# A signal of its own for the gate half of every up step in a macaron block on one core

## The chip, the cores and the metric

The kernel runs on one core of a Trainium2 chip. Time is device time of one execution, in microseconds (us). The engines of the core run side by side and meet only through semaphores: TensorE (PE) multiplies, ScalarE (ACT) and VectorE (DVE) work on what it leaves in PSUM, GpSimd (POOL) does small things here, SyncE (SP) issues most transfers.

## What is computed

The block is a feed-forward, an attention and the same feed-forward again, each behind a layer norm and with a residual, on 4096 tokens of 512 features in fp32. Cut to what matters (einsums written short):

```python
def _L0_ffn_ref(x, W1, W2, W3):            # hidden width 2048
    up_gate = x @ W1.T
    up_lin = x @ W3.T
    hidden = silu(up_gate) * up_lin
    hidden = fwht(hidden)                  # Walsh-Hadamard over 2048
    return hidden @ W2.T

x = x + 0.5 * _L0_ffn_ref(_layernorm(x), W1, W2, W3)
x = x + _L0_attn_ref(_layernorm(x), wq, wk, wv, wo, inv_freq)
x = x + 0.5 * _L0_ffn_ref(_layernorm(x), W1, W2, W3)
```

The attention mixes the 16 heads of one token with each other (16 x 16 scores for a token), so no token looks at another one.

## The kernel before

**Tiles and passes.** A tile is 512 tokens, so there are 8 tiles, and each goes twice through the feed-forward. These are the 16 passes of `PASSES`, p = 0 to 15. Pass 0 (`first_pass`) also builds the weights, with the Hadamard transform folded into W2. Passes 1 to 15 are `feed_forward(p)` on every engine, and between two of them lies a gap (`first_gap`, `early_gap`, `late_gap`, and for the last pass `last_gap` on DVE), in which PE makes queries, keys, values and attention outputs for one to three blocks of 128 tokens.

**A step.** A pass has 16 steps of 128 hidden features, n = 0 to 15, with two buffers each, u = n % 2. In an *up step* PE makes both halves of a step in PSUM: `w = 0` is the gate, in bank `gu[:, 2u]`, and `w = 1` is the linear half, in bank `gu[:, 2u+1]`. Every product is three matmuls (`products`, lines 583 to 585: high by high, high by low, low by high, to get fp32 out of the fast format), so with 4 blocks of the contraction a half is 12 matmuls and a step 24. Then ACT computes silu of the gate into `gated` (L1031; L976 in pass 0), DVE multiplies `gated` by the linear half in place (L1525; L1407), ACT copies the product as the high part into `hid` (L1039), and DVE takes the low part as the difference (L1532). In a *down step* PE multiplies high and low by W2 into the four banks of `acc` (L614, L615 and L618; in the last down step of a pass by `products`).

**Order.** The order on each engine is written out by hand. On PE it is up(n), down(n-1), up(n+1), down(n), so that a down step lies between the end of an up step and the next. On DVE the two feed-forward instructions of a step stand in a row with everything else that it does: units of attention (a product over 1024 elements, L1258 or L1263, and a sum, L1270 or L1272), norms, and the shift and the sums of the softmax (L1278, L1279, L1286, L1287). On ACT the exponential of the softmax (L955) stands between the silu and the copy of some steps; silu and exponential each need their table loaded (ACT_TABLE_LOAD).

**Semaphores around the change.** `s_up_done` counts up steps: the last matmul of a step, of the half w = 1, raises it. ACT's silu waits for it and for the buffer `gated` to be free; SP's loads of the next up weights wait for it; in pass 0, so does the split of the next raw weights on ACT. DVE's product waits for `s_silu` alone. `s_h` counts the products, `s_hid_hi` and `s_hid_lo` the two parts. PE waits for `s_h` of two steps before it writes over a pair of banks in `gu`.

**The end of a pass.** Step 15 has no attention unit. Where the next pass's new tile is prepared beside this one, DVE does behind L1532: the low part of new blocks (L1138), two subtractions on the new tile's input (L1510), and then in the gap `add_sum` (L1202: residual plus `acc`) for s = 0, the statistics of one new block, `add_sum` for s = 1 to 3 and the block's norm (L1174). In the gaps of passes 2, 9 and 11 the second new block isn't ready earlier, and PE transposes it (L664) between the query and the key product of the first, as soon as that norm is there. In the other gaps both blocks were normed in the pass before.

Of the kernel before, what the change touches and what calls it, by code (L numbers as in the profile page):

```python
# [246 lines left out]
def build(nc, x, up_raw, w2t, attn_raw, inv_freq, hadamard, identity, out):  # L247
    ctx = ExitStack()
    with ctx:
# [3 lines left out]
        def sem(name):  # L253
            return ctx.enter_context(nc.semaphore(name))
# [65 lines left out]
        s_w_hi = sem("s_w_hi")  # L320
        s_wattn = sem("s_wattn")

        s_up_done = sem("s_up_done")
        s_silu = sem("s_silu")
        s_h = sem("s_h")
# [39 lines left out]
        def raw_hidden(n):  # L365

            at = RAW.index(n)
            if at < 2 * SUBS:
                return xs[2 + at // SUBS][:, at % SUBS, :]
            return prod[:, 2, (at - 2 * SUBS) * TOK:(at - 2 * SUBS + 1) * TOK]  # L370
# [21 lines left out]
        def residual(t):  # L392

            return xs[t % 4]
# [24 lines left out]
        def by_token(ap):  # L419
            return ap.rearrange("p (s q j) -> p s q j", s=SUBS, q=QUADS)  # L420

        def from_bank(ap, p):

            if p in MOVED:
                return ap.rearrange("p (q s j) -> p s q j", q=QUADS, s=SUBS)
            return by_token(ap)
# [153 lines left out]
        def _(pe):  # L580
            def products(o, w_hi, w_lo, m_hi, m_lo, first, last):

                nc.tensor.matmul(o, w_hi, m_hi, start=first, stop=False)  # L583
                nc.tensor.matmul(o, w_hi, m_lo, start=False, stop=False)  # L584
                return nc.tensor.matmul(o, w_lo, m_hi, start=False, stop=last)  # L585

            def split_ready(*key):

                pe.wait_ge(s_tp_lo, TP[key] + 1)

            def up(u, X, key=None):
                for w in range(2):
                    for k in range(KT):
                        if key == NP - 1:
                            if (w, k) == (0, 0):
                                for s in range(SUBS):
                                    split_ready("z", s, 0)
                        elif key in MOVED:
                            if w == 0 and k % 2 == 0:
                                pe.wait_ge(s_moved_lo, 2 * MOVED[key] + k // 2 + 1)  # L600
                        elif key is not None and w == 0:
                            split_ready("x", key, k)
                        ins = products(gu[:, 2 * u + w, :], w_up[:, u, 0, w, k, :], w_up[:, u, 1, w, k, :],
                                       X[:, 0, k, :], X[:, 1, k, :], k == 0, k == KT - 1)
                ins.then_inc(s_up_done, 1)

            def down(n, u, first, last, slab=None, split=None):
                hi, lo = (w_down[:, u, 0, :], w_down[:, u, 1, :]) if slab is None else slab
# [284 lines left out]
            for s in range(SUBS):  # L893
                pe.wait_ge(s_ln, s + 1)
                for k in range(KT):
                    ins = nc.tensor.transpose(gu[:, k, s * P:(s + 1) * P], xs[2][:, s, k * P:(k + 1) * P], ident[:])
# [15 lines left out]
        def _(act):  # L912
# [54 lines left out]
            up_high(1, 0, 1, False)  # L967
            for n in range(HT):
                u = n % 2
                act.wait_ge(s_up_done, n + 1)  # L970
                if n >= 2:
                    if n - 2 < SPLIT_FIRST:
                        act.wait_ge(s_hid_lo, n - 1)
                    else:
                        act.wait_ge(s_h, n - 1)
                nc.scalar.activation(gated[:, u, :], gu[:, 2 * u, :], ACT.Silu).then_inc(s_silu, 1)  # L976
                if n + 2 < HT:
                    up_high(n + 2, n // 2 + 1, u, True)
                for part, a in hadamard_batch(n):
                    act.wait_ge(s_had_ps, HT * part + a + 1)  # L980
                    nc.scalar.activation(down_stage[:, a, PARTS[part]], acc[:, a % BATCH, PARTS[part]], ACT.Copy, scale=DOWN_SCALE)\
                        .then_inc(s_down_hi, 1)
                if n < SPLIT_FIRST:
                    act.wait_ge(s_h, n + 1)
                    nc.scalar.activation(hidden_0(n)[0], gated[:, u, :], ACT.Copy).then_inc(s_hid_hi, 1)
                if n == 2:
                    act.dma_start(tok[:, :, W2_CUTS[2]], w2t[:, :, W2_CUTS[2]].rearrange("a p n -> p a n")).then_inc(s_w2[2], 16)
# [36 lines left out]
            def feed_forward(p):  # L1024

                n0, after = HT * p, p + 1
                for n in range(HT):
                    u = n % 2
                    act.wait_ge(s_up_done, n0 + n + 1)
                    act.wait_ge(s_hid_lo, n0 + n - 1)  # L1030
                    nc.scalar.activation(by_token(gated[:, u, :]), from_bank(gu[:, 2 * u, :], p), ACT.Silu).then_inc(s_silu, 1)  # L1031
                    for g in EXP_AHEAD.get((p, n), ()):
                        exp(g)
                    if n == HT - 1 and after == NP - 1:
                        for s in range(2):
                            block_high("o", s, (after + 1) % 2)
                    act.wait_ge(s_h, n0 + n + 1)
                    act.wait_ge(s_down_done, n0 + n - 1)
                    nc.scalar.activation(hidden(u)[0], gated[:, u, :], ACT.Copy).then_inc(s_hid_hi, 1)  # L1039
                    if n == HT - 1 and after < NP and after not in LATE:  # L1040
                        for g in early_subs(after):
                            sub_high(g)
                    for g in EXP_BEHIND.get((p, n), ()):
                        exp(g)
                    if after in MOVED and X_MOVE <= n < X_MOVE + QUADS:
                        move(after, n - X_MOVE)
                    if after in MOVED and n == X_SPLIT:
                        moved_high(after)
                    f, t = PASSES[p - 1]
                    if f == 2 and n == 1:  # L1050
                        act.wait_ge(s_added, SUBS * p)
                        act.dma_start(out_v[t], residual(t)[:]).then_inc(s_out, 16)
                    if f == 2 and n == 4 and t + 4 < TILES:
                        act.wait_ge(s_out, 16 * (t + 1))
                        act.dma_start(residual(t + 4)[:], x_v[t + 4]).then_inc(s_x[t % 2], 16)
# [67 lines left out]
        def _(dve):  # L1123
# [280 lines left out]
            for n in range(HT):  # L1404
                u = n % 2
                dve.wait_ge(s_silu, n + 1)
                nc.vector.tensor_tensor(raw_hidden(n) if n in RAW else gated[:, u, :], gated[:, u, :], gu[:, 2 * u + 1, :], ALU.mult)\  # L1407
                    .then_inc(s_h, 1)
                turn(1)
                if n + 2 < HT:  # L1410
                    up_low(n + 2, u)
                for part, a in hadamard_batch(n):
                    at = HT * part + a
                    dve.wait_ge(s_down_hi, at + 1)
                    cols = PARTS[part]
                    nc.vector.scalar_tensor_tensor(down_stage[:, a, D + cols.start:D + cols.stop], acc[:, a % BATCH, cols], DOWN_SCALE,
                                                   down_stage[:, a, cols].bitcast(FP32), ALU.mult, ALU.subtract).then_inc(s_down_lo, 1)
                if n < SPLIT_FIRST:
                    dve.wait_ge(s_hid_hi, n + 1)
                    high, low = hidden_0(n)  # L1420
                    nc.vector.tensor_tensor(low, gated[:, u, :], high.bitcast(FP32), ALU.subtract).then_inc(s_hid_lo, 1)
                turn(1)
# [41 lines left out]
            def feed_forward(p):  # L1464

                n0, after = HT * p, p + 1
# [55 lines left out]
                for n in range(HT):  # L1522
                    u, count = n % 2, len(STEP_UNITS[p][n])
                    dve.wait_ge(s_silu, n0 + n + 1)
                    nc.vector.tensor_tensor(by_token(gated[:, u, :]), by_token(gated[:, u, :]), from_bank(gu[:, 2 * u + 1, :], p), ALU.mult).then_inc(s_h, 1)  # L1525
                    unit(min(count, 1))
                    if n == HT - 1 and after == NP - 1:
                        for s in range(2):
                            block_low("o", s, (after + 1) % 2)
                    dve.wait_ge(s_hid_hi, n0 + n + 1)  # L1530
                    high, low = hidden(u)
                    nc.vector.tensor_tensor(low, gated[:, u, :], high.bitcast(FP32), ALU.subtract).then_inc(s_hid_lo, 1)  # L1532
                    unit(count - min(count, 1))
                    if n == HT - 1 and next_x:
                        for g in early:
                            sub_low(g)
                    beside(n)
# [144 lines left out]
```

## Time and profile before

| | us |
|---|---|
| runs before | 2517.53, 2519.74, 2520.30 |
| median | 2519.74 |
| the profiled execution | 2519.57 |
| its span | 2517.8 |
| outside the span | 1.8 |
| PE busy | 2504.8 |
| DVE busy | 2027.5 |
| ACT busy | 528.8 |

The mean granted clock of TensorE over the span is 0.999 of full speed. A row of matmuls shows each of them as about 0.39 us long while the next one begins 0.227 us after it, since they overlap; what counts is the distance from one start to the next. The idle time that the profile gives for PE begins only at the modelled end of the matmul before.

### The profile page before, as it was taken

To read this page: it belongs to the slowest core of one execution; us is meant where nothing else is said; L and a number is where in the kernel's file an instruction comes from. 1 tells how busy PE (TensorE), PEld (TensorE's weight loads), DVE (VectorE), ACT (ScalarE), POOL (GpSimd) and SP (SyncE) were. 2 spreads that over 40 slices of the span, in tenths; PEclk is the share of its full clock that TensorE was granted. 3 is DMA by queue.
4 is the path that set the end of the run, shared out by engine and by line. 5 is a ranking of instruction groups with operands and counts; after the bars stand their busy time and mean duration, and the time that the engine had idled before them with its cause. 6 is when DMAs were issued, how large, how long until landed. Compare 5 with 4: busy or idle time off the path is not lost.

```text
span 2517.8 us, 30105 instructions
## 1 busy us (share of the span) xinstructions
PE 2504.8 (99%) x11223; PEld 2074.0 (82%) x11223; DVE 2027.5 (81%) x2588; ACT 528.8 (21%) x810; POOL 63.6 (3%) x111
## 2 busy tenths in 40 slices
PE   9999999999999999999999999999999999999999
PEld 7878888888888888888888888888888888888887
DVE  9558978799786997979969889697886988978711
ACT  3322221222121221122212222122221212211211
POOL 0030000000000000000000000000000000000000
PEclk9999999999999999999999999999999999999999
DMA  9644635256452454525625546354562545535364
GB/s 340 251 188 177 213 138 190 101 199 202 169 207 76 176 210 162 203 100 200 203 89 208 167 180 211 118 213 146 200 208 76 186 165 210 185 115 200 134 219 165
DMA packets 112404, 446.89 MB, mean 177 GB/s; under 512 B 11201, under 2 KB 36033, under 8 KB 79041
## 3 DMA queue, kind: packets, MB, share of 16 engines
q1 hardware_dynamic: 82080, 420.26, 45.8%
q10 hardware_dynamic: 30240, 25.57, 3.4%
q8 instruction: 47, 0.77, 0.1%
q14 instruction: 37, 0.29, 0.0%
HBM read 402.79 MB, written 33.55 MB: 173 GB/s over the span
## 4 chain that ended last, share of the span: by engine, by line
PE 95%; DVE 4%; DMA 1%; ACT 0%; issue 0%; SPq 0%; DVEq 0%; ACTq 0%
PE gu L583 21%; PE gu L584 21%; PE gu L585 21%; PE acc L615 8%; PE acc L614 8%; PE acc L618 8%; PE acc L583 2%; PE acc L585 2%; PE acc L584 2%; PE acc L644 1%; DMA prod<-up_raw 1%; PE acc L709 1%; DVE prod L1263 1%; DVE mixed L1272 0%; DVE x L1202 0%; DVE w_up L1323 0%
## 5 line engine op out<-in xcount | busy, mean ns | idle before, releaser
L583 PE MATMUL gu<-xt,w_up 128*128 128x512 f32 x2048 | 798.6, 390 | 0.6 <-DVE xt L1138 0.4
L585 PE MATMUL gu<-xt,w_up 128*128 128x512 f32 x2048 | 796.9, 389 | 0.0
L584 PE MATMUL gu<-xt,w_up 128*128 128x512 f32 x2048 | 796.7, 389 | 0.0
L583 PEld LDWEIGHTS gu<-xt,w_up 128*128 128x128 f32 x2048 | 384.5, 188 | 81.6 <-issue 1.5
L584 PEld LDWEIGHTS gu<-xt,w_up 128*128 128x128 f32 x2048 | 384.5, 188 | 79.7
L585 PEld LDWEIGHTS gu<-xt,w_up 128*128 128x128 f32 x2048 | 384.5, 188 | 79.6
L1031 ACT ACTIVATE gated<-gu 128x512 f32<-128x512 f32 x240 | 143.6, 599 | 1137.8 <-PE gu L585 1137.8
L1525 DVE TENSOR_TENSOR gated<-gated,gu 128x512 f32<-128x512 f32 x240 | 163.2, 680 | 271.8 <-ACT gated L1031 271.2
L614 PE MATMUL acc<-w_down,hid 128*128 128x512 f32 x896 | 349.4, 390 | 0.0
L615 PE MATMUL acc<-w_down,hid 128*128 128x512 f32 x896 | 348.6, 389 | 0.0
L1258 DVE TENSOR_TENSOR prod<-tok 128x1024 f32<-128x1024 f32 x256 | 309.0, 1219 | 0.9
L1272 DVE TENSOR_REDUCE mixed<-prod 128x64 f32<-128x1024 f32 x256 | 309.6, 1211 | 0.0
L1270 DVE TENSOR_REDUCE scores<-prod 128x32 f32<-128x1024 f32 x256 | 309.2, 1211 | 0.0
L1263 DVE TENSOR_TENSOR prod<-scores,tok 128x1024 f32<-128x1024 f32 x256 | 307.4, 1212 | 1.5 <-DVE head_sum L1287 0.2
L618 PE MATMUL acc<-w_down,hid 128*128 128x512 f32 x896 | 239.5, 389 | 0.0
L1039 ACT ACTIVATE hid<-gated 128x512 fp32r<-128x512 f32 x240 | 151.8, 633 | 365.6 <-DVE gated L1525 365.2
L618 PEld LDWEIGHTS acc<-w_down,hid 128*128 128x128 f32 x896 | 168.2, 188 | 34.9
L614 PEld LDWEIGHTS acc<-w_down,hid 128*128 128x128 f32 x896 | 168.2, 188 | 34.7
L615 PEld LDWEIGHTS acc<-w_down,hid 128*128 128x128 f32 x896 | 168.3, 188 | 34.6
L1532 DVE TENSOR_TENSOR hid<-gated,hid 128x512 fp32r<-128x512 f32 x240 | 163.9, 683 | 20.3 <-ACT hid L1039 20.3
L583 PE MATMUL gu<-w_attn,sub_xt 128*128 128x512 f32 x232 | 91.2, 393 | 0.0
L585 PE MATMUL gu<-w_attn,sub_xt 128*128 128x512 f32 x232 | 90.3, 389 | 0.0
(141 smaller groups left out, 1956.0 us busy)
## 6 DMA issues: line engine op xcount, KB each, us to landing
w_up<-up_pairs SPq DMA_DIRECT2D x240, 1024.0 KB, 4.8
w_down<-down_pairs SPq DMA_DIRECT2D x240, 512.0 KB, 3.4
up_pairs<-w_up SPq DMA_DIRECT2D x16, 1024.0 KB, 4.9
xt<-tok ACTq DMA_DIRECT2D x144, 64.0 KB, 4.1
prod<-up_raw SPq DMA_DIRECT2D x16, 512.0 KB, 6.1
down_pairs<-w_attn SPq DMA_DIRECT2D x4, 2048.0 KB, 18.1
out<-x ACTq DMA_DIRECT2D x7, 1024.0 KB, 5.9
x<-x ACTq DMA_DIRECT2D x6, 1024.0 KB, 7.3
```

Of the source, the lines that this page charges most:

```text
L583: nc.tensor.matmul(o, w_hi, m_hi, start=first, stop=False)
L584: nc.tensor.matmul(o, w_hi, m_lo, start=False, stop=False)
L585: return nc.tensor.matmul(o, w_lo, m_hi, start=False, stop=last)
L614: nc.tensor.matmul(acc[:, s, :], h_hi[:, s * P:(s + 1) * P], hi, start=first, stop=False)
L615: nc.tensor.matmul(acc[:, s, :], h_hi[:, s * P:(s + 1) * P], lo, start=False, stop=False)
L618: ins = nc.tensor.matmul(acc[:, s, :], h_lo[:, s * P:(s + 1) * P], hi, start=False, stop=False)
L1258: return nc.vector.tensor_tensor(prod[:, buf, :].rearrange("p (h t d) -> p h t d", h=2, t=HEADS), wide(q[:, h:h + 2, None, :], 2, HEADS), ...
L1263: return nc.vector.tensor_tensor(prod[:, buf, :].rearrange("p (h d t) -> p h d t", h=2, d=HD), wide(scores[:, g % 2, h:h + 2, None, :], 2, ...
L1270: return nc.vector.tensor_reduce(scores[:, g % 2, h:h + 2, :], prod[:, buf, :].rearrange("p (h t d) -> p h t d", h=2, t=HEADS), AX.X, ALU.add)
L1272: return nc.vector.tensor_reduce(mixed[:, h:h + 2, :], prod[:, buf, :].rearrange("p (h d t) -> p h d t", h=2, d=HD), AX.X, ALU.add)
L1525: nc.vector.tensor_tensor(by_token(gated[:, u, :]), by_token(gated[:, u, :]), from_bank(gu[:, 2 * u + 1, :], p), ALU.mult).then_inc(s_h, 1)
L1532: nc.vector.tensor_tensor(low, gated[:, u, :], high.bitcast(FP32), ALU.subtract).then_inc(s_hid_lo, 1)
```

## The change

There is a new semaphore `s_gate_done`. On PE the last matmul of the gate half raises it, and the last matmul of the linear half raises `s_up_done` as before. On ACT the silu waits for `s_gate_done` in place of `s_up_done`, in pass 0 and in all others. On DVE the product waits for `s_silu` and in addition for `s_up_done`. No instruction of any engine changes its place: there are as many of them on PE, ACT and DVE as before, in the same order, and only these waits and signals differ. The loads on SP wait as they did.

```diff
@@ build
+        s_gate_done = sem("s_gate_done")
         s_up_done = sem("s_up_done")
@@ block.tensor, up
                         ins = products(gu[:, 2 * u + w, :], w_up[:, u, 0, w, k, :], w_up[:, u, 1, w, k, :],
                                        X[:, 0, k, :], X[:, 1, k, :], k == 0, k == KT - 1)
-                ins.then_inc(s_up_done, 1)
+                    ins.then_inc(s_gate_done if w == 0 else s_up_done, 1)
@@ block.scalar, pass 0
-                act.wait_ge(s_up_done, n + 1)
+                act.wait_ge(s_gate_done, n + 1)
@@ block.scalar, feed_forward
-                    act.wait_ge(s_up_done, n0 + n + 1)
+                    act.wait_ge(s_gate_done, n0 + n + 1)
@@ block.vector, pass 0
                 dve.wait_ge(s_silu, n + 1)
+                dve.wait_ge(s_up_done, n + 1)
@@ block.vector, feed_forward
                     dve.wait_ge(s_silu, n0 + n + 1)
+                    dve.wait_ge(s_up_done, n0 + n + 1)
```

## Rows read from the trace of the kernel before

**Rows 1.** The page, part 1: busy time, share of span and instructions of each engine

```profile
PE 2504.8 (99%) x11223; PEld 2074.0 (82%) x11223; DVE 2027.5 (81%) x2588; ACT 528.8 (21%) x810; POOL 63.6 (3%) x111
```

**Rows 2.** The page, part 4: the chain that ended last, by engine

```profile
PE 95%; DVE 4%; DMA 1%; ACT 0%; issue 0%; SPq 0%; DVEq 0%; ACTq 0%
```

**Rows 3.** The waits of PE: line, waited for, us in total, times, longest

```profile
PE gu L583 <- DVE tok L1241: 2.5, 1, 2.5
PE gu L664 <- DVE prod L1174: 2.4, 3, 0.8
...
PE acc L583 <- DVE hid L1532: 1.0, 2, 0.8
```

**Rows 4.** The page, part 5: silu and product, busy, mean ns, idle before, releaser

```profile
L1031 ACT ACTIVATE gated<-gu 128x512 f32<-128x512 f32 x240 | 143.6, 599 | 1137.8 <-PE gu L585 1137.8
L1525 DVE TENSOR_TENSOR gated<-gated,gu 128x512 f32<-128x512 f32 x240 | 163.2, 680 | 271.8 <-ACT gated L1031 271.2
```

**Rows 5.** Timeline in pass 3: start, us, engine, line; an up step's end

```profile
609.73 0.39 PE L585 MATMUL gu<-xt,w_up 128*128 128x512 f32 x1
...
609.96 0.39 PE L614 MATMUL acc<-w_down,hid 128*128 128x512 f32 x1
```

**Rows 6.** Timeline, end of pass 1 and gap of pass 2 (ACT, DVE, PE)

```profile
315.31 0.60 ACT L1031 ACTIVATE gated<-gu 128x512 f32<-128x512 f32 x1 [3.93 <-PE gu L585]
...
315.95 0.69 DVE L1525 TENSOR_TENSOR gated<-gated,gu 128x512 f32<-128x512 f32 x1 [0.87 <-ACT gated L1031]
...
314.88 0.39 PE L585 MATMUL gu<-xt,w_up 128*128 128x512 f32 x1
...
323.59 0.39 PE L585 MATMUL gu<-w_attn,sub_xt 128*128 128x512 f32 x1
324.71 0.66 PE L664 MATMUL gu<-ident,prod 128*128 128x128 f32 x4 [0.74 <-DVE prod L1174]
```

**Rows 7.** Timeline of pass 10 from its step 12 to its end (ACT, DVE, PE)

```profile
1712.43 0.42 ACT L955 ACTIVATE scores<-scores 128x256 f32<-128x256 f32 x1
...
1710.42 0.43 DVE L1279 TENSOR_TENSOR scores<-scores,head_max 128x256 f32<-128x256 f32 x1
...
1712.88 0.42 DVE L1286 TENSOR_REDUCE head_sum<-scores 128x16 f32<-128x256 f32 x1 [1.04 <-ACT scores L955]
...
1735.86 0.68 DVE L1525 TENSOR_TENSOR gated<-gated,gu 128x512 f32<-128x512 f32 x1
...
1734.58 0.39 PE L585 MATMUL gu<-xt,w_up 128*128 128x512 f32 x1
```

**Rows 8.** Timeline, last two steps of pass 9 (DVE, PE)

```profile
1567.70 0.42 DVE L1286 TENSOR_REDUCE head_sum<-scores 128x16 f32<-128x256 f32 x1 [1.04 <-ACT scores L955]
...
1577.04 0.69 DVE L1532 TENSOR_TENSOR hid<-gated,hid 128x512 fp32r<-128x512 f32 x1 [0.70 <-ACT hid L1039]
...
1576.01 1.07 PE L618 MATMUL acc<-w_down,hid 128*128 128x512 f32 x4
1577.88 0.47 PE L583 MATMUL acc<-w_down,hid 128*128 128x512 f32 x1 [0.80 <-DVE hid L1532]
```

**Rows 9.** Timeline, the last down step of the kernel (PE)

```profile
2510.27 1.07 PE L618 MATMUL acc<-w_down,hid 128*128 128x512 f32 x4
2511.51 0.47 PE L583 MATMUL acc<-w_down,hid 128*128 128x512 f32 x1 [0.17 <-DVE hid L1532]
```

**Rows 10.** Timeline and chain in pass 0 (DVE, and a load of raw weights)

```profile
18.20 0.69 DVE L1407 TENSOR_TENSOR gated<-gated,gu 128x512 f32<-128x512 f32 x1 [0.47 <-ACT gated L976]
...
33.39 8.75 DMA prod<-up_raw
```

**Rows 11.** Timeline in the first gap: DVE reads `gu` while PE writes it

```profile
168.93 0.66 DVE L1230 TENSOR_TENSOR prod<-gu,cos_t 128x512 f32<-128x512 f32 x1
...
169.05 0.39 PE L584 MATMUL gu<-w_attn,xt 128*128 128x512 f32 x1
169.28 0.39 PE L585 MATMUL gu<-w_attn,xt 128*128 128x512 f32 x1
```

## The prediction

> **What bounds the kernel now.** I read the busy times first, then the chain that ended last, then PE's own waits, and only then stretches of the timeline. PE is busy for 2504.8 us of a span of 2517.8 us, and DVE for 2027.5 [rows 1]; 95% of the chain that ended last is PE [rows 2]. So an edit that gives PE neither fewer matmuls nor shorter ones can win only where PE stands still, and by the profile that is 2517.8 - 2504.8 = 13.0 us in the whole span. The large numbers elsewhere mislead: silu has 1137.8 us of idle time before it, all put down to PE, and DVE's product 271.2 us put down to silu [rows 4]. Both are idle time of engines that are not the bound. What the change is worth has to be read at the few places where PE waits for something that hangs on a silu.
>
> PE's waits [rows 3] are a short list. The longest, 2.5 us, is for the rotated queries in the first gap (L1241), whose input comes from PE's own query and key matmuls and from the norm of the second tile; no silu is in it, so it stays. Then there are three of 2.4 us together, one in each of the gaps of passes 2, 9 and 11 (L664 waits for the norm L1174), and two of 1.0 us together at a last down step, which waits for the low part L1532. These five hang on the last steps of a pass, where DVE works off a row of instructions behind the product. The rest of the 13.0 us lies at the start, in pass 0, and in the tail behind PE's last matmul.
>
> **What is added.** Every one of the 256 up steps gets a second signal, in the middle of it, and DVE's product a second wait. For the signal the nearest row is the one that exists: the last matmul of an up step carries a signal already, and the next matmul begins 609.96 - 609.73 = 0.23 us after it [rows 5], the same distance as between any two. I take 0. For a price above nothing I take the mark that a wait leaves on PE: the first matmul behind one took 0.47 us against 0.39 [rows 8], so 0.08 us a step, 256 x 0.08 = 20.5 us, is the upper end if the signal broke up the stream of matmuls. Below nothing it can't be, since a signal takes no work away.
>
> A rule speaks against the change here. The trace shows no cost of a signal on PE [rows 5]. The Trainium skill, page "TensorE: Matmul & The Clock Gate", section "Why this matters for your kernels", has the tail of a group of matmuls grow by 26.3 ns for each semaphore increment and advises a single one on the last. If each of the 256 new ones cost that on the path, it would be an estimated 6.7 us, which the gain summed below would not cover.
>
> The second thing that is new is that ACT reads the gate bank while PE writes its neighbour; before, PE was writing `acc` by then. The nearest row is in the first gap, where DVE reads two banks of `gu` from 168.93 on and PE writes a third: its matmuls begin at 169.05 and 169.28, 0.23 us apart [rows 11]. I take 0, and no gain is possible from it.
>
> The second wait on DVE can only hold the product until the linear half is there, which silu's own wait did before. What is queued behind the product on DVE (attention units, L1532, the softmax) therefore starts no later than before, but for the handling of one more wait. DVE has 2517.8 - 2027.5 = 490 us without work [rows 1], so that is covered except in the chains below, where it costs some hundredths of a us each.
>
> **What is moved.** The gate half is done 12 matmuls before the linear half, 12 x 0.227 = 2.7 us earlier. Silu takes 0.60 us [rows 4], so where ACT is free it is over before the linear half is, and the product begins right after PE's last matmul in place of silu's time later. The gain per step on the way to the product is therefore not 2.7 but about 0.65 us, and less where DVE was late anyway.
>
> - *Gap of pass 2.* The last matmul of step 15 begins at 314.88 and ends at 315.27; silu began at 315.31, the product at 315.95, with 0.87 us of idle time before it [rows 6]. The product can begin at about 315.30: 0.65 us. Everything between it and the norm L1174 is DVE, or ACT's copy, back to back, so the norm moves by the same 0.65. PE's transposes began 324.71 - 323.59 = 1.12 us after the matmul before [rows 6], 0.89 more than the distance of 0.227, so all of the 0.65 arrives. Next late is the same norm, by 0.24 us. Gain 0.65.
> - *Gap of pass 9.* The same row of work and a wait of the same kind, one of the three of 2.4 us in all [rows 3]. Gain 0.65.
> - *Gap of pass 11.* Here the product of step 15 waited for no silu: it began at 1735.86, 0.89 us after the linear half (1734.58 + 0.39), since DVE was busy [rows 7]. The delay is older. In step 12 the exponential ran at 1712.43, behind the silu and a table load, and DVE stood still for 1.04 us before the row sums at 1712.88; the shift that the exponential needs was ready at 1710.42 + 0.43 = 1710.85. With silu 2.7 us earlier the table is loaded by then, the exponential ends near 1711.3, and the row sums can begin when the product of step 12 is done, about 1711.5. DVE is then over 1.3 us ahead for three steps, and the product of step 15 begins at its earliest, 1735.0: a gain of 0.86.
> - *End of pass 9.* The low part of step 15 began at 1577.04, and PE's last down step at 1577.88; from the row sums at 1567.70 on DVE was busy until the product of step 15, and before them it stood still for the exponential for 1.04 us again [rows 8]. With both silus out of the way DVE is more than 1.3 us ahead, and the wait goes. It is worth more than the 0.80 us shown: the fourth of the matmuls from 1576.01 on begins at 1576.69, so the distance is 1.19 us, 0.96 over 0.227, and 0.08 for the slow first matmul. Gain 1.04.
> - *The tail.* In the last pass DVE is free and the low part is bound to PE, silu, product, copy. The distance from 2510.27 + 3 x 0.227 = 2510.95 to 2511.51 is 0.56 [rows 9], 0.33 over the normal one, and with 0.08 as above 0.41; silu's 0.65 covers it. Gain 0.41.
> - *Pass 0.* The first product waited 0.47 us for its silu at 18.20 [rows 10], and DVE works without a pause for long after it. But what reaches PE goes through loads of raw weights, one of them 8.75 us long for 0.5 MB [rows 10] in the stretch where the transfers are densest. So the gain is between 0 and 0.47; I take 0.2, since a load that starts earlier among full queues doesn't have to end earlier.
>
> Sum: 0.65 + 0.65 + 0.86 + 1.04 + 0.41 + 0.2 = 3.8 us. Against the profiled execution of 2519.57 us that is 2515.8; the median of the runs is 2519.74, 0.2 above it, and I stay at 2515.8. It is 0.15%.
>
> **The rivals.** *Only a part arrives.* If a chain has a second reason to be late (the copy on ACT, the rstd on POOL, or the exponential that isn't there sooner), the two gains that rest on an older delay, 0.86 and 1.04, fall away, and with pass 0 at nothing 1.7 us are left: 2517.9. Against it speaks that DVE's rows stand back to back between the two ends of those chains; for it, that I put two stalls down to an exponential eleven to twenty-five us before.
>
> *More arrives than I count.* A wait of PE below 0.16 us (0.39 - 0.227) is invisible in the idle times, and at the ends of the other passes the same chain is as long. With some ten pass ends left and up to 0.16 us at each, 1.6 us more would be there, and with the whole 0.47 of pass 0 the time is 2513.9. The hard floor is all idle time of PE gone, 2519.57 - 13.0 = 2506.6, which the start and the tail exclude. A gain beyond 5 us would need a silu on the path at a place that I hold to be free of it.
>
> *Slower: the signal in the middle of the stream.* If the matmul behind a signal that another engine waits for begins late, every up step pays. At the 0.08 us from above it is 20.5 - 3.8 = 16.7 us more: 2536.3. It decides from (5.0 + 3.8) / 256 = 0.034 us a step on. Against it stands that the signal at the end of a step costs none of that [rows 5]; for it, only that no row has one between two halves whose weights come from the same buffer.
>
> The Trainium skill's 26.3 ns from the page above would make an estimated 2522.5 us here, so slower, but inside the bound of what can be told.
>
> *The change doesn't do what it says.* Silu could still begin late if its second wait, for the buffer `gated` (the low part of two steps before), were the later one. At the places that count that low part is several us old, so this would give the time of before, 2519.6; I count it with the first rival.
>
> **How the numbers follow.** A measurement of this kernel can tell about 0.2%, or 5.0 us, from no change. The forecast, a gain between 2.5 and 5.0 us, has 0.62; only a part (0 to 2.5 us) 0.17; more than 5.0 us 0.16; the signal or the read of the neighbour bank costs more than is gained 0.05, of which 0.03 lies beyond 5.0 us. So faster by over 0.2% has 0.16, within 0.2% has 0.81, slower 0.03. The range leaves out the slower case and the outer half of both neighbours: 2513.0 to 2519.0, with 0.2 us added above for the median against the profiled execution, 2519.2.
>
> **What would show it.** In the profile after, silu should have only PE before it and begin about 2.7 us before the end of an up step, and the product's idle time should be put down to PE, no longer to ACT. PE's waits on the norm L1174 should be one or two of 0.1 us or so, where they were three of 0.8, and those on L1532 should be gone. The 2.5 us wait on L1241 stays. The distance from one matmul to the next at the middle and at the end of an up step should be 0.227 us; anything above 0.03 us more at the middle makes the forecast wrong. It would also be wrong if DVE's 1.04 us before the row sums stayed.

## The result and the profile after

| | before | after |
|---|---|---|
| median of 15 runs each, us | 2519.67 | 2515.01 |
| lowest to highest | 2517.53 to 2520.74 | 2513.11 to 2517.02 |
| ratio, 95% interval | | 0.9983 (0.9976 to 0.9990) |
| profiled execution, us | 2519.57 | 2516.34 |
| its span | 2517.8 | 2514.6 |

The change makes the kernel 4.66 us faster by the medians, 0.19%; the ratio gives 0.17% with 0.10% to 0.24% around it. That is just under the 5.0 us (0.2%) from which a gain was to be called clear, and the far end of the interval reaches beyond it. The prediction was 2515.8, with 2513.0 to 2519.2 around it and 0.81 on "within 0.2%".

One thing has to be known to read single runs. The runs of either kernel fall into two groups that differ in the mean granted clock of TensorE, listed as 1.0 or 0.999. Of the 33 runs of before that ran beside the first four experiments, 15 with 1.0 have a mean of 2517.97 us and 18 with 0.999 one of 2519.73. Of the changed kernel's 15 runs, 6 with 1.0 have a mean of 2513.83 and 9 with 0.999 one of 2515.76. Within a group the gain is 4.1 and 4.0 us; against the 31 runs of before beside the next four experiments (means 2518.32 and 2519.55) it is 4.5 and 3.8, so these means are good to some 0.4 us. What lies between the groups is shown further down. Two runs, one of before and one of e9_stats, took 4242 us at a mean granted clock of 0.556 and are left out of every comparison.

The busy times, for [rows 1], and silu and product, for [rows 4] (line numbers are up by one to three):

```profile
PE 2503.4 (100%) x11223; PEld 2074.9 (83%) x11223; DVE 2027.7 (81%) x2588; ACT 531.8 (21%) x810; POOL 63.6 (3%) x111
...
L1528 DVE TENSOR_TENSOR gated<-gated,gu 128x512 f32<-128x512 f32 x240 | 163.4, 681 | 266.8 <-PE gu L586 266.1
...
L1032 ACT ACTIVATE gated<-gu 128x512 f32<-128x512 f32 x240 | 143.7, 599 | 634.1 <-PE gu L586 632.0
```

No engine has more or fewer instructions than before. Silu's idle time went from 1137.8 to 634.1 us and the product's is put down to PE and no longer to silu; but the product still idles for 266.8 us, where it was 271.8. Reading the gain off those rows would have given hundreds of us, or nothing. PE's waits, for [rows 3], tell it:

```profile
PE gu L584 <- DVE tok L1242: 2.6, 1, 2.6
PE gu L897 <- DVE x L1175: 2.0, 1, 2.0
PE acc L889 <- DVE hid L1329: 1.9, 1, 1.9
PE gu L665 <- DVE prod L1175: 0.7, 3, 0.2
PE acc L710 <- DVE carrier L1135: 0.6, 1, 0.6
```

The two waits of 1.0 us for the low part are gone and the three for the norm fell from 2.4 to 0.7 us. The wait for the rotated queries stays (2.5 before, 2.6 now). The wait before the very first transposes (L897) is 2.0 us, where it was 0.7 (L896 in before): DVE stood idle for the input tile's transfers there, 1.15 us for the last of them, before any silu had run. That hides part of the gain in this profile.

The gap of pass 2, for [rows 6] (timeline: start, us, engine, line):

```profile
313.06 0.60 ACT L1032 ACTIVATE gated<-gu 128x512 f32<-128x512 f32 x1 [1.77 <-PE gu L586]
...
315.85 0.69 DVE L1528 TENSOR_TENSOR gated<-gated,gu 128x512 f32<-128x512 f32 x1 [0.87 <-PE gu L586]
...
315.35 0.39 PE L586 MATMUL gu<-xt,w_up 128*128 128x512 f32 x1
...
324.00 0.39 PE L586 MATMUL gu<-w_attn,sub_xt 128*128 128x512 f32 x1
324.62 0.66 PE L665 MATMUL gu<-ident,prod 128*128 128x128 f32 x4 [0.23 <-DVE prod L1175]
```

Silu now begins 2.3 us before the last matmul of the step does, and the product begins 0.50 us after that matmul's start, where it was 1.07 (314.88 to 315.95). From there on everything is as it was, only earlier, and PE's pause is 0.62 us from start to start in place of 1.12. The matmuls between the two places (the last down step and the query product) took 0.06 us less as well, so the whole 0.56 us arrives.

PE's instructions are the same in number and order in every variant, so the traces can be laid over each other matmul by matmul. From pass 1 on before and after then differ by more than 0.1 us at just six places. The distance from the start of one matmul to the next there, in us (0.227 is normal):

| place | before | after | silu late (e3) | step 15 only (e5) | steps 0 to 14 only (e6) |
|---|---|---|---|---|---|
| gap of pass 2 | 1.12 | 0.62 | 1.13 | 0.62 | 1.18 |
| end of pass 7 | 0.34 | 0.23 | 0.35 | 0.35 | 0.23 |
| gap of pass 9 | 1.16 | 0.61 | 1.15 | 0.61 | 1.15 |
| end of pass 9 | 1.19 | 0.23 | 1.19 | 1.18 | 0.23 |
| gap of pass 11 | 1.24 | 0.62 | 1.21 | 1.21 | 1.15 |
| last down step | 0.56 | 0.23 | 0.56 | 0.23 | 0.56 |

Before minus after is 0.50 + 0.11 + 0.55 + 0.96 + 0.62 + 0.33 = 3.1 us. More lies around the places: behind a wait at the end of a pass the next distance was 0.31 us and is 0.23 now, and at the end of pass 10 a distance of 0.29 and such a slow one are gone too (0.15 us together). Counted from the last up matmul of the pass to eleven matmuls behind each place, before minus after is 0.56, 0.23, 0.58, 1.08, 0.77 and 0.45 us, 3.7 in all. The whole is read from the end of pass 1 to PE's last matmul, first of before, then of after:

```profile
2514.12 0.39 PE L585 MATMUL acc<-w_down,hid 128*128 128x512 f32 x1
```

```profile
2510.89 0.39 PE L586 MATMUL acc<-w_down,hid 128*128 128x512 f32 x1
```

From 314.88 [rows 6] to 2514.12 it is 2199.24 us, from 315.35 to 2510.89 it is 2195.54: PE's stream is 3.70 us shorter in between. This length, to be called the stream below, can be read in every trace, and it doesn't move with the arrival of the first tiles.

### The profile page after: what moved, and what is told of

The parts are those of the page before. It is cut to its first block, busy times and chain, and to the rows that moved or that the text cites. A ratio compares the mean times of both kernels' runs of the same rounds, so it can differ in the third digit from the quotient of the medians.

```text
span 2514.6 us, 30351 instructions
## 1 busy us (share of the span) xinstructions
PE 2503.4 (100%) x11223; PEld 2074.9 (83%) x11223; DVE 2027.7 (81%) x2588; ACT 531.8 (21%) x810; POOL 63.6 (3%) x111
## 4 chain that ended last, share of the span: by engine, by line
PE 96%; DVE 3%; DMA 1%; ACT 0%; issue 0%; SPq 0%; DVEq 0%
PE gu L584 21%; PE gu L585 21%; PE gu L586 21%; PE acc L615 8%; PE acc L616 8%; PE acc L619 8%; PE acc L584 2%; PE acc L586 2%; PE acc L585 2%; PE acc L645 1%; PE acc L710 1%; DVE x L1203 0%; DVE tok L1363 0%; DMA prod<-up_raw 0%; DVE tok L1356 0%; DVE w_up L1324 0%
## 5 line engine op out<-in xcount | busy, mean ns | idle before, releaser
L1528 DVE TENSOR_TENSOR gated<-gated,gu 128x512 f32<-128x512 f32 x240 | 163.4, 681 | 266.8 <-PE gu L586 266.1
L1032 ACT ACTIVATE gated<-gu 128x512 f32<-128x512 f32 x240 | 143.7, 599 | 634.1 <-PE gu L586 632.0
```

## The experiments

All of them are edits of the changed kernel. Each label's clock groups are compared where medians alone would mislead.

### The signals and waits alone (e3_signals)

```diff
-                act.wait_ge(s_gate_done, n + 1)
+                act.wait_ge(s_up_done, n + 1)
@@ passes 1 to 15
-                    act.wait_ge(s_gate_done, n0 + n + 1)
+                    act.wait_ge(s_up_done, n0 + n + 1)
```

> The change with silu put back: the gate half still raises its own semaphore, DVE's product still waits for both, but silu waits for the end of the up step in every pass, as before. Theory (signals and waits are free, the gain is silu's earlier start): the median of before, 2519.7, within 1 us; PE's stalls in the gaps of passes 2, 9 and 11 stay at 1.12, 1.16 and 1.24 us from start to start, within 0.1. Rival (a signal in the middle costs 0.01 us or more a step and the rest of the change is worth more than seen): 2.5 us or more above before.

2518.84 us against 2519.03 of before on the same chip, ratio 1.0001 (0.9992 to 1.0010). All six distances are as before to 0.03 us (table), and the stream is 2199.26 us, where before has 2199.24. So the second signal of each step, and a second wait on DVE that has long been met when the first one ends, cost nothing that can be measured, and the whole gain comes from silu's earlier start.

### Six more signals in every step (e4_incs)

```diff
+        s_probe = sem("s_probe")
@@ up
+                        if k < KT - 1:
+                            ins.then_inc(s_probe, 1)
                     ins.then_inc(s_gate_done if w == 0 else s_up_done, 1)
```

> The change with six more signals in each up step: the last matmul of each of the first three blocks of the contraction in both halves raises a semaphore for which nobody waits, 1536 more in all. Theory (a signal costs PE nothing): the time of the changed kernel, 2515.0 within 1.5 us, and 0.227 us from start to start behind each. Rival (26.3 ns for each, the Trainium skill's estimate in the page TensorE: Matmul & The Clock Gate): 40 us more, 2555.

2515.34 us, ratio to before 0.9986 (0.9977 to 0.9995): the time of the changed kernel. The stream is 2195.57 us, where the changed kernel has 2195.54. A signal after every third matmul leaves it as it is; in the timeline of PE in this run L587 is the matmul that carries one:

```profile
1000.05 0.39 PE L587 MATMUL gu<-xt,w_up 128*128 128x512 f32 x1
1000.28 0.39 PE L585 MATMUL gu<-xt,w_up 128*128 128x512 f32 x1
1000.51 0.39 PE L586 MATMUL gu<-xt,w_up 128*128 128x512 f32 x1
1000.73 0.39 PE L587 MATMUL gu<-xt,w_up 128*128 128x512 f32 x1
1000.96 0.39 PE L585 MATMUL gu<-xt,w_up 128*128 128x512 f32 x1
```

From 1000.05 to 1000.28 and from 1000.73 to 1000.96 it is 0.23 us, as everywhere. The estimate of 40 us falls. What the Trainium skill states in the page "TensorE: Matmul & The Clock Gate", section "Why this matters for your kernels", is a tail behind a group of matmuls. In the stream of this run, which goes on behind each signal, nothing of it shows.

### Pass 0 alone, and the other passes alone (e1_pass0, e2_rest)

```diff
@@ e1_pass0, passes 1 to 15
-                    act.wait_ge(s_gate_done, n0 + n + 1)
+                    act.wait_ge(s_up_done, n0 + n + 1)
@@ e2_rest, pass 0
-                act.wait_ge(s_gate_done, n + 1)
+                act.wait_ge(s_up_done, n + 1)
```

> Silu starts early in pass 0 alone; in passes 1 to 15 it waits for the end of the up step. Theory: the jumps of PE's stream that I count in the profile after (0.51, 0.20, 0.55, 0.96, 0.62 and 0.33 us, 3.2 us in all) lie in passes 1 to 15, so pass 0 is worth 0 to 0.5 us: 2519.2 to 2519.7. Rival (the measured 4.66 us hold more than those 3.2 because pass 0 gains over 1 us through earlier loads): 2518.7 or less.

> Silu starts early in passes 1 to 15 alone; pass 0 is as before. Theory: 3.2 to 4.2 us faster than before, 2515.5 to 2516.5, with the same six jumps in PE's stream. Rival (pass 0 carries over 1 us, or only the clock in pass 0 differs): 2.5 us faster or less.

e1: 2518.38, ratio 0.9998 (0.9989 to 1.0007). e2: 2515.22, ratio 0.9986 (0.9977 to 0.9995), and its six distances are those of the changed kernel. Within the clock groups (1.0, then 0.999) the mean of e1 is 0.0 us (2517.93 against 2517.97) and 0.6 us (2519.14 against 2519.73) below before, that of e2 3.4 us (2514.55) and 4.1 us (2515.65). So passes 1 to 15 carry the gain, and pass 0 has between nothing and about 0.6 us. By the medians both expectations were missed: e1 lies 0.8 us below its range and inside that of the rival (2518.7 or less), e2 0.3 us below its own. 7 of the 11 runs of e1 have the clock of 1.0, against 15 of 33 of before, so only the groups and the traces tell the two theories apart. The stream is 2199.19 us in e1 and 2195.58 in e2.

The traces narrow pass 0 down. Before 46 us the arrival of the first loads shifts PE by more than the change does. But from PE's 206th matmul (46.11 in before) to the one ahead of the long wait in the first gap (169.96), the five executions with silu late in pass 0 (before, e2, e3, e5, e6) take 123.85 to 123.91 us, and the eight with silu early 123.60 to 123.73. That is 0.2 us, and the two ranges don't meet.

### Step 15 alone, and the other steps alone (e5_last, e6_others)

```diff
@@ both, pass 0
-                act.wait_ge(s_gate_done, n + 1)
+                act.wait_ge(s_up_done, n + 1)
@@ e5_last, passes 1 to 15
-                    act.wait_ge(s_gate_done, n0 + n + 1)
+                    act.wait_ge(s_gate_done if n == HT - 1 else s_up_done, n0 + n + 1)
@@ e6_others, passes 1 to 15
-                    act.wait_ge(s_gate_done, n0 + n + 1)
+                    act.wait_ge(s_up_done if n == HT - 1 else s_gate_done, n0 + n + 1)
```

> Silu starts early only in step 15 of passes 1 to 15, and late in all other steps. Theory: the gains that I put down to step 15 alone stay (0.51 us at the gap of pass 2, 0.55 at that of pass 9, 0.33 at the last down step), those that I put down to an older delay behind an exponential go: at the end of pass 9 the distance from start to start stays 1.19 us, less at most 0.1, and in the gap of pass 11 it stays 1.24, less at most 0.3. About 1.5 us faster than before. Rival (step 15 alone carries them all): the same six jumps as in the changed kernel.

> Silu starts early in steps 0 to 14 of passes 1 to 15 and late in step 15. Theory: the mirror of the run before: 0.96 us at the end of pass 9 stays, as DVE is ahead there; at the gaps of passes 2 and 9 and at the last down step nothing is gained (1.12 and 1.16 us from start to start, 0.56 at the end); at the gap of pass 11 the product of step 15 now waits for its silu, so of the 0.62 us at most 0.3 are left. About 1.3 us faster than before. Rival (the older delay is not the exponential's): nothing at the end of pass 9.

e5: 2517.51, ratio 0.9995 (0.9985 to 1.0005), e6: 2518.53, ratio 0.9997 (0.9986 to 1.0007), before 2519.17. The times can't be told from before, but the streams and the table can: e5's stream is 2197.67 us and e6's 2197.74, 1.57 and 1.50 us shorter than before's, where about 1.5 and 1.3 were expected. Their sum is 0.6 us short of the 3.7, mostly since one place needs both halves. Step 15 alone gives the gaps of passes 2 and 9 and the last down step. The other steps alone give the end of pass 9, of pass 7, and the 0.15 us at the end of pass 10. The gap of pass 11 needs both: 1.21 with the one, 1.15 with the other, 0.62 with both. DVE at the end of pass 9, first in e5, then in e6:

```profile
1563.79 0.69 DVE L1528 TENSOR_TENSOR gated<-gated,gu 128x512 f32<-128x512 f32 x1 [1.14 <-ACT gated L1032]
1565.52 0.42 DVE L1287 TENSOR_REDUCE head_sum<-scores 128x16 f32<-128x256 f32 x1 [1.04 <-ACT scores L956]
```

```profile
1564.96 0.69 DVE L1528 TENSOR_TENSOR gated<-gated,gu 128x512 f32<-128x512 f32 x1 [1.15 <-PE gu L586]
1565.56 0.41 DVE L1287 TENSOR_REDUCE head_sum<-scores 128x16 f32<-128x256 f32 x1
```

With the silu of step 14 late, DVE stands still behind the product for 1.04 us until the exponential is there; with it early, the row sums follow the product at once. PE feels it some 10 us later, at the last down step. Of the 32 row sums in a trace, five have this 1.04 us of idle time before them in before, e3 and e5, and none in the changed kernel and e6. The reason given for the two "older delays" holds.

### The two waits in the other order (e7_swap)

```diff
-                    dve.wait_ge(s_silu, n0 + n + 1)
-                    dve.wait_ge(s_up_done, n0 + n + 1)
+                    dve.wait_ge(s_up_done, n0 + n + 1)
+                    dve.wait_ge(s_silu, n0 + n + 1)
```

(and the same in pass 0)

> The change with the two waits before DVE's product in the other order, the linear half first and silu second. In the profile after, the product began 0.50 us after the start of the step's last matmul, where silu before began 0.43 us after it. Theory (the order decides which wait stands in front as an instruction of its own, and the one in front costs some hundredths when it is the late one): 0.44 to 0.47 us, or 0.53 and more. Rival (0.50 is what DVE needs from a signal of PE, whatever stands in front): 0.50 within 0.01.

The product at the end of pass 1 and the matmul before it:

```profile
315.77 0.69 DVE L1528 TENSOR_TENSOR gated<-gated,gu 128x512 f32<-128x512 f32 x1 [0.87 <-PE gu L586]
...
315.34 0.39 PE L586 MATMUL gu<-xt,w_up 128*128 128x512 f32 x1
```

0.43 us, as silu before. It is not one case: of the 215 up steps in the trace that a down step follows, 92 have 0.50 in the changed kernel, and here over 90 have 0.43. Each of the three gaps' distances is 0.07 us shorter too (0.54 to 0.55). So the order of two waits is worth 0.07 us where the late one is the one that matters. The rival's 0.50 falls; 0.43 lies just below the range of the theory, and why the order matters is not shown. PE's three waits for the norm are 0.5 us together, where they were 0.7:

```profile
PE gu L665 <- DVE prod L1175: 0.5, 3, 0.2
```

That is 0.2 us of the kernel's time, which the times can't show; the one run took 2516.26.

### What is still late: the norm in the gaps (e8_norm)

```diff
@@ early_gap on DVE
                 for s in range(1, SUBS):
+                    if s == SUBS - 1 and just:
+                        sub_norm(just[0])
                     add_sum(p - 1, s)
                 if just:
-                    sub_norm(just[0])
```

> The change, and in the gaps of passes 2, 9 and 11 DVE makes the norm of the second block ahead of the last of the four additions, in place of behind it. Theory (what is still late in those gaps after the change is that norm, 0.62 us from start to start where 0.227 is normal): the three distances fall to 0.227 and PE gains 3 x 0.39 = 1.2 us: 2513.8 against 2515.0. Rival (POOL's rstd arrives only then, so that the norm can't run earlier): no change, and DVE idle before the norm.

2514.05 us, ratio to before 0.9978 (0.9969 to 0.9988). PE has no wait for the norm any more in any of the three gaps; the distances fell by another 0.39 us each, to 0.23, and GpSimd's part of the norm (the rival) holds nothing up. Against the changed kernel it is 1.4 us within the one clock group (2514.34 and 2515.76) and 1.2 us in the other (2512.67 and 2513.83), where 1.2 was worked out. The stream is 2194.28 us, 1.26 shorter than the changed kernel's.

### The long wait in the first gap (e9_stats, e12_stats_o)

```diff
@@ e9_stats and e12_stats_o, DVE behind pass 0
             sub_low(1)
-            sub_low(2)
             dve.wait_ge(s_second_x, 16)
             for s in range(SUBS):
                 at = ln_stats(("x", 1), s, xs[1][:, s, :])
             ln_means(("x", 1), at, ("b", SUBS - 1))
+            sub_low(2)
@@ e12_stats_o alone, ACT behind pass 0
-            for g in new_subs(1):
+            for g in new_subs(1)[:2]:
                 sub_high(g)
             weight_high(O, 0)
             weight_high(O, 1)
+            sub_high(new_subs(1)[2])
```

> The change, and in the first gap DVE takes the statistics of the second tile (2.85 us, L1161 and L1169) ahead of the low part of the third block, where it stood idle for 5.3 us, and no longer between that and the first rope. Theory (the one long wait of PE hangs on this row of DVE work and on no silu): PE's wait of 2.6 us for the rotated queries goes, and with it the clock, which in the profile of before fell to 1.2 GHz right behind that wait for 3.4 us, has no reason to fall there: 2.5 to 4 us below the changed kernel, 2511.0 to 2512.5, and less scatter among the runs. Rival (the query and key matmuls or POOL's rstd hold the chain as much): the wait stays above 1.5 us and the time within 1 us of 2515.0.

A miss. 2514.80 us, ratio 0.9981 (0.9972 to 0.9991), within the noise of the changed kernel. The numbers are those of the rival (a wait above 1.5 us, the time within 1 us of 2515.0), but not its mechanism: the rope (the rotation of queries and keys, L1231 to L1242) did come 2.8 us earlier in PE's stream, and then ran into something that neither theory had. DVE and GpSimd in e9 (timeline):

```profile
167.98 0.68 DVE L1231 TENSOR_TENSOR prod<-gu,cos_t 128x512 f32<-128x512 f32 x1
168.70 0.70 DVE L1241 TENSOR_TENSOR tok<-prod 128x256 f32<-128x256 f32 x1
169.33 1.50 DVE L1242 TENSOR_TENSOR tok<-prod 128x256 f32<-128x256 f32 x1
170.76 1.48 DVE L1241 TENSOR_TENSOR tok<-prod 128x256 f32<-128x256 f32 x1
172.16 0.41 DVE L1242 TENSOR_TENSOR tok<-prod 128x256 f32<-128x256 f32 x1
...
166.57 5.38 POOL L1116 TENSOR_TENSOR w_attn<-tok,w_attn 128x512 fp32r<-128x512 f32 x4 [7.22 <-ACT w_attn L999]
```

The three of the four additions that fall before the end of GpSimd's subtractions at 171.95 take 0.70, 1.50 and 1.48 us; the fourth takes 0.41. The subtractions took longer too, 5.38 us, where they took 5.03 in the changed kernel and 5.04 in e12. The wait of PE is still 2.2 us. So e12 moved GpSimd's work away as well.

> The kernel with the statistics moved (run e9_stats), and ACT makes the high part of the last attention weight ahead of the third block's split in the first gap, in place of behind it, so that GpSimd's four subtractions (L1116) run some 5 us earlier. Theory (in e9_stats the rope came early and then ran into GpSimd: L1241 and L1242, additions of SBUF with SBUF, took 0.7 to 1.5 us in place of 0.42, only while L1116 ran): they take 0.42 us again, PE's wait of 2.2 us before the third query falls below 0.3, and the time is 2 us below e9_stats, about 2512.5. Rival (those additions are slow for what PE or the transfers do at that time): they stay slow at the same place, the wait stays near 2.2 us, 2514.8.

2511.46 us, ratio to before 0.9968 (0.9956 to 0.9980), 1 us below what was expected. The same additions in e12, and GpSimd:

```profile
168.30 0.43 DVE L1242 TENSOR_TENSOR tok<-prod 128x256 f32<-128x256 f32 x1
168.64 0.42 DVE L1243 TENSOR_TENSOR tok<-prod 128x256 f32<-128x256 f32 x1
168.97 0.42 DVE L1242 TENSOR_TENSOR tok<-prod 128x256 f32<-128x256 f32 x1
169.31 0.42 DVE L1243 TENSOR_TENSOR tok<-prod 128x256 f32<-128x256 f32 x1
...
160.23 5.04 POOL L1117 TENSOR_TENSOR w_attn<-tok,w_attn 128x512 fp32r<-128x512 f32 x4 [1.24 <-ACT w_attn L999]
```

The wait is gone from PE's list: the matmul that waited now begins at 169.84, behind one at 169.62. Within the clock group 1.0, e12 has a mean of 2511.60 and e9 of 2514.04, 2.4 us apart, which is the wait. The medians are 3.3 us apart, and the clock is the reason for the rest: all 6 runs of e12 have a mean clock of 1.0, against 2 of the 10 of before beside them. Here is the stretch with the long wait and what follows it, of before and then of e3_signals, whose PE stream is the same there (by stretch: length, busy time and count on PE, PEld, DVE, ACT and POOL, granted clock, DMA share, GB/s):

```profile
170.00:180.00 10.00, 7.46 (x26) 5.74 (x25) 8.54 (x19) 0.00 (x0) 2.96 (x4) 0.83 0.23 86
```

```profile
170.00:180.00 10.00, 7.45 (x37) 5.85 (x36) 9.36 (x20) 0.03 (x1) 3.78 (x4) 1.00 0.34 129
```

In before the granted clock is half, 1.2 GHz, for 3.4 us from the end of the wait of 2.54 us on: the matmuls there stand 0.43 us apart and not 0.23, 1.6 us in all. In e3, behind a wait of 2.55 us, it stayed at 2.4 GHz. The two groups of before lie 1.76 us apart, so this is most likely what lies between them. Of the ten profiled executions with a wait of 2.5 us or more there, five have such a stretch behind it (before, e4, e6, e7, e8), and the changed kernel's has one at the start, behind the 2.0 us for the late first tile; the other four have none. Over all runs, a mean clock of 0.999 came in 18 of 33, 21 of 31 and 8 of 10 of before, in 9 of 15 of the changed kernel, in 6 of 10 of e9 (a wait of 2.2 us), and in 1 of 11 of the two kernels without the wait (e12, e13). So the change under study shows no part in it.

### All together (e13_all)

> The change, the statistics and the last attention weight moved as in e12_stats_o, and the norm of the gaps moved as in e8_norm. Theory (the stalls are apart from each other, so the gains add): 1.1 us below e12_stats_o, about 2511.5, 8 us or 0.3% below before. Rival (a stall taken out early comes back as a wait elsewhere): within 0.5 us of e12_stats_o.

The edits of e12 and e8 on the changed kernel give 2509.93 us (2509.39 to 2511.95), ratio to before 0.9963 (0.9949 to 0.9976): 9.8 us faster than before, 1.5 less than e12. 2511.5 had been expected, as e12 was taken at 2512.5; the step from e12 was to be 1.1. Within the clock group 1.0 it is 8.8 us faster than before (2509.80 and 2518.60) and 1.8 less than e12. The gains add up. What is left of PE's waits:

```profile
PE acc L889 <- DVE hid L1330: 1.9, 1, 1.9
PE acc L710 <- DVE carrier L1136: 0.7, 1, 0.7
PE gu L897 <- DVE x L1176: 0.6, 1, 0.6
```

All of it lies before 60 us; behind that no distance from one start to the next is above 0.48 us.

## Why the prediction was right, point by point

- **What bounds the kernel.** Right: PE's stream is the same, and all that changed is where it stops. The list of PE's waits named five of the six places.
- **Price of the signals and waits.** Right at 0 for the signals (e3, e4): behind the last matmul of a gate half the next one begins 0.227 us later, as everywhere. The Trainium skill's estimated 6.7 us, for which 2522.5 stood, didn't come. The "some hundredths" for the second wait on DVE were 0.07 us, and they hang on something that the working missed: the order of the waits (e7).
- **Gaps of passes 2 and 9.** 0.65 each was to come; 0.50 and 0.55 came in the gaps, 0.56 and 0.58 with the matmuls around them. The product was to begin where silu had begun, 0.43 us after the start of the last matmul; it began at 0.50, by the order of the waits, so it moved by 0.57 only.
- **Gap of pass 11.** 0.86 was to come; 0.62 came in the gap and 0.15 at the end of pass 10 just before it, 0.77 together. The product of step 15 began 1.28 us after the start of the last matmul and now begins at 0.50, in place of the 0.42 that was forecast. The mechanism held (e5 and e6: neither half alone is enough); the term was 0.09 too large, again by the order of the waits. That a part would arrive ahead of the gap was not said.
- **End of pass 9.** 1.04 was to come; 0.96 is in the distance, and with the slow matmul behind the wait it is 1.08. Right, and e5 and e6 show the exponential as its reason.
- **Tail.** 0.41 was to come, 0.33 is in the distance, 0.45 with the slow matmul behind it. Right.
- **Pass 0.** 0.2 in a span of 0 to 0.47. The times give 0 to 0.6 (e1), the traces 0.2 behind 46 us. What it is worth before that is open, since the arrival of the first loads shifts each execution there by more.
- **Not counted.** 0.11 us at the end of pass 7, hidden below the 0.16 us that PE's idle times can't show, and 0.12 in the slow matmuls behind it; it is the rival "more arrives" in small. The other ends of passes had nothing above 0.1 in one distance.
- **Signs.** PE's waits on the norm were to be one or two of 0.1 us or so; three of up to 0.2 are left, 0.07 us by the order of the waits and 0.06 since the matmuls ahead of them went faster. The rest came as said: no wait on the low part, the product's idle time put down to PE, and the 1.04 us before the row sums gone.

From the end of pass 1 on the terms make 0.65 + 0.65 + 0.86 + 1.04 + 0.41 = 3.6 us, and PE's stream became 3.7 us shorter. That the two agree to 0.1 is in part luck: the three gaps came out 0.25 us too large together, and the end of pass 7, which wasn't counted, gave 0.23. With pass 0 the traces show 3.9 us, and the clock groups 3.8 to 4.5. The medians' 4.66 us lie 0.6 above the 4.0 and 4.1 us within the groups; which runs got the lower clock may be part of it, and how much was not settled.

## What to carry to other kernels

Where one engine is busy for 99% of the span, the idle times of all others say nothing of what an edit brings; list the bound engine's own waits and follow each back, past the instruction it waits for, to the last place where that chain stood still. That place can be three steps and thirty us earlier (the exponential of step 12 in pass 10, 1712.43, for PE's stop in the gap of pass 11, 1743.38), on another engine. When the waits are settled, ask of each what the next-late thing is, since it caps the gain. And where an instruction waits for two semaphores, try both orders: here the one with the late wait written first was 0.07 us better.

## What the runs showed that was not expected

- Additions on DVE with both inputs in SBUF (128x256) took 0.70 to 1.50 us while GpSimd made subtractions from SBUF (e9), and 0.41 to 0.43 us without them (e12). Products on DVE that read PSUM took 0.68 us, under GpSimd's work and without it. What is gained by moving DVE work into an idle hole can thus be lost again at once.
- The order of two waits before one DVE instruction moved its start by 0.07 us (0.50 and 0.43 us after the start of the last matmul), in over 90 steps of each kernel.
- Behind a wait of PE of 2.5 us the granted clock fell from 2.4 to 1.2 GHz for 3.4 us in five of ten profiled executions whose PE stream was the same there; behind the waits of 0.8 us it did in none.
